# Experts' tiles of a fused attention and mixture-of-experts kernel: rows normalised one tile ahead, turned behind the second chunk, rounded in front of the activations, an expert read once on TensorE

## What is computed

```python
x = x + _L0_xattn_ref(ctx_1024, _layernorm(x), ...)
gate_scores = softmax(z @ Wg + bg)                # z = _layernorm(x)
top1 = argmax(gate_scores)                        # one expert of 8 for a token
h = silu(z @ W1[e] + b1[e])                       # 256 -> 1024
y = (h @ W2[e] + b2[e]) * gate_scores[top1]       # 1024 -> 256
x = x + y
```

## Time and profile before

| | before |
|---|---|
| runs, median (lowest to highest) | 2175.25 us (2172.24 to 2176.8) |
| profiled execution, device time | 2173.39 us |
| profiled execution, first to last instruction (span) | 2171.7 us |
| mean granted TensorE clock | 0.975 of full speed |
| busy share of the span: PE, DVE, ACT, POOL | 93%, 74%, 68%, 65% |
| first tile gathered | 1899.15 us |
| last tile's scatter begins | 2162.61 us |

### The profile page before, as it was taken

One profiled execution on the slowest core, in us unless ns is written; L12 is line 12 of the kernel. 1 busy time (PEld: TensorE's weight loads), 2 busy tenths in 40 slices (PEclk: granted clock), 3 DMA queues, 4 the chain that ended last, 5 costly groups with the idle time before them and its releaser, 6 DMA issues. The chain is left out here.

```text
span 2171.7 us, 63039 instructions
## 1 busy us (share of the span) xinstructions
PE 2010.2 (93%) x25468; PEld 1367.3 (63%) x25468; DVE 1615.2 (74%) x3115; ACT 1472.5 (68%) x1835; POOL 1421.1 (65%) x803
## 2 busy tenths in 40 slices
PE   2799999999999999999999999999999998589997
PEld 2266666667666666667666666676666665567675
DVE  7677777777778888777788887777888874745554
ACT  4277777776677777766777777767777777156664
POOL 3078888884688877865877788748878877023232
PEclk9699999999999999999999999999999999789999
DMA  5122222222222222222222222222222221271110
GB/s 167 37 53 53 53 54 63 53 55 59 68 58 54 53 53 53 59 54 70 53 58 63 54 53 53 49 71 54 62 54 54 53 62 28 94 302 37 44 44 27
DMA packets 127505, 137.92 MB, mean 64 GB/s; under 512 B 45538, under 2 KB 92310, under 8 KB 126070
## 3 DMA queue, kind: packets, MB, share of 16 engines
q1 hardware_dynamic: 123477, 124.49, 22.3%
q0 software_dynamic: 3744, 9.39, 1.4%
HBM read 53.06 MB, written 26.15 MB: 36 GB/s over the span
## 5 line engine op out<-in xcount | busy, mean ns | idle before, releaser
L708 POOL TENSOR_TENSOR probs_split<-probs,probs_split 128x1024 f16<-128x1024 f32 x576 | 1222.8, 2136 | 363.2 <-ACT probs_split L793 362.1
L786 ACT ACTIVATE probs<-score 128x1024 f32<-128x1024 f32 (+1 forms) x640 | 655.9, 1025 | 397.4 <-PE score L1076 386.8
L931 DVE TENSOR_REDUCE max_parts<-aux 128x1 f32<-128x512 f32 x1024 | 683.1, 688 | 101.7 <-PE aux L1076 93.5
L793 ACT ACTIVATE probs_split<-score 128x1024 f16<-128x1024 f32 (+1 forms) x640 | 652.0, 1019 | 0.0
L1172 PE MATMUL acc<-values,probs_split 128*128 128x65 f16 x5120 | 554.7, 193 | 8.2 <-POOL probs_split L708 8.0
L1176 PE MATMUL acc<-values,probs_split 128*128 128x64 f16 x4608 | 519.8, 194 | 0.0
L1177 PE MATMUL acc<-values,probs_split 128*128 128x65 f16 x4608 | 517.6, 192 | 0.0
L1172 PEld LDWEIGHTS acc<-values,probs_split 128*128 128x128 f16 x5120 | 464.0, 97 | 64.5 <-POOL probs_split L708 11.7
L1076 PE MATMUL score<-q_both,k_high 128*128 128x512 f16 (+1 forms) x1280 | 485.7, 379 | 10.6 <-DMA q_max<-max_row 7.8
L1076 PE MATMUL aux<-k_high,q_both 128*128 128x512 f16 (+1 forms) x1536 | 461.9, 335 | 33.0 <-DVE values L927 20.6
L1076 PE MATMUL score<-q_max,k_low 65*128 65x512 f16 (+1 forms) x1280 | 488.6, 382 | 0.0
(11 more groups left out here) (170 smaller groups left out, 2242.7 us busy)
## 6 DMA issues: line engine op xcount, KB each, us to landing
k_high<-raw SPq DMA_DIRECT2D x128, 147.2 KB, 2.5
q_both<-raw SPq DMA_DIRECT2D x128, 128.0 KB, 2.5
piece_in<-in_L_ffn_W SPq DMA_DIRECT2D x64, 256.0 KB, 3.1
halves<-piece_out SPq DMA_DIRECT2D x128, 128.0 KB, 2.4
k_low<-raw SPq DMA_DIRECT2D x64, 147.2 KB, 2.4
q_max<-raw SPq DMA_DIRECT2D x64, 128.0 KB, 2.5
w<-halves SPq DMA_DIRECT2D x16, 512.0 KB
w<-halves SPq DMA_DIRECT2D x8, 1024.0 KB
```

Source lines behind the costliest of these rows:

```text
L708: nc.gpsimd.tensor_tensor(out=low[0:r, :], in0=prob(h, j)[0:r, :], in1=high[0:r, :], op=ALU.subtract)\
L786: nc.scalar.activation(prob(h, j)[0:r, :], score[j % 2][0:r, :], ACT.Exp, scale=SCALE)\
L793: nc.scalar.activation(halves(h, j)[0][0:r, :], score[j % 2][0:r, :], ACT.Exp, scale=SCALE)\
L931: nc.vector.tensor_reduce(max_parts[g % 2][:, t, c:c + 1], bank[:, :], AX.X, ALU.max)\
```

## The change

PE turns tile `k + 2` behind chunk 1 and no longer behind chunk 4. It reads each tile's expert once, behind that `turn`, and keeps it until the tile is done: four reads to a group where five stood. ACT rounds the turned rows of `k + 2` (`z_high_half`) ahead of the first half of `hidden_layer` of `k + 1`, no longer behind it. DVE normalises tile `k + 3` and no longer `k + 2` in the step of tile `k`, and does it behind the first half of `hidden_low` of `k + 1` and right ahead of `finish` of `k`; tile 2 is normalised ahead of the loop. POOL's and SP's programs are as they were.

```diff
+    TURN_AT = 1
@@ ACT
                 hidden_layer(i, u, 1)
+                z_high_half(i, u + 2)
                 hidden_layer(i, u + 1, 0)
-                z_high_half(i, u + 2)
@@ DVE
             z_low_half(0, 1)
+            normalise_rows(0, 2)
             hidden_low(0, 0, 0)
             dve.wait_ge(b2_loaded, 16)
             def step(i, u):
                 hidden_low(i, u, 1)
-                normalise_rows(i, u + 2)
                 z_low_half(i, u + 2)
                 hidden_low(i, u + 1, 0)
+                normalise_rows(i, u + 3)
                 finish(i, u)
@@ PE
-            e = expert_of(0, 0)
+            experts_of = {0: expert_of(0, 0)}
             for c in range(KF):
-                upward(0, 0, e, c)
-            experts_of = {}
+                upward(0, 0, experts_of[0], c)
+            experts_of[1] = expert_of(0, 1)
             def step(i, u):
                 more = exists(i, u + 1)
-                if u == 0:
-                    experts_of[0], experts_of[1] = expert_of(i, 0), expert_of(i, 1)
+                k = number(i, u)
                 for c in range(KF):
                     if more:
-                        upward(i, u + 1, experts_of[u + 1], c)
-                    downward(i, u, experts_of[u], c)
-                    if c == BANK:
+                        upward(i, u + 1, experts_of[k + 1], c)
+                    downward(i, u, experts_of[k], c)
+                    if c == TURN_AT:
                         turn(i, u + 2)
-                        if u + 2 <= OWN and exists(i, u + 2):
-                            experts_of[u + 2] = expert_of(i, u + 2)
+                        if exists(i, u + 2):
+                            experts_of[k + 2] = expert_of(i, u + 2)
```

## The result

The changed kernel takes 2214.3 us (median of 4 runs, 2212.62 to 2214.76), the kernel before beside it 2174.84 us. The ratio is 1.0181, with a 95% interval from 1.0163 to 1.0198: 39 us slower. The forecast was 2221 us.

A forecast was written before the change was run, and what follows sets the result against it. PE set the pace before; a ring through DVE and the gather would now, at 7.58 us a tile. 48.2 us late at tile 35, less 2.3, gives 45.9 us on 2175.25: 2221 us, range 2205 to 2230.

The forecast's parts named there:

- The ring: DVE's finish waits behind the gather that the previous tile's outputs free; 7.58 us a tile, bounds 6.7 and 7.9.
- The sum: Ring links 0.83 + 1.32 + 3.07 + 0.95 + 1.41 = 7.58 us a tile, over PE's 6.19 us.
- The landing: Link from the gather's start on POOL to its landing: 3.07 us, the mean of 30 gathers; median 2.8.
- Normalise to finish: Link on DVE from normalise to finish's first instruction, the expert's read between: 0.95 us; other bound some 0.35 us.
- The two ends of the sum: Before the 31 links: tile 4's outputs 9.3 us late; after tile 35: some 2.3 us less than before's 16.8.
- Part one: PE, one register read fewer in four tiles: gain of 0.69 us per four tiles, some 6 us; bounds 0 to 6.
- Parts two and three: PE's turn moved behind chunk 1, and ACT's rounding ahead of the activations: each forecast to cost nothing by itself.
- Where PE would wait: PE's downward matmuls at chunk 4 stop for DVE's second half of hidden_low, about 1.4 us for each tile.
- the clock: Rival: PE's stops lower its clock, 7.8 us a tile, up to 16 us more, 2237 us; chance 0.10.
- The short ring: Rival: same ring, expert's read overlapping normalisation and fewer long landings; 6.7 to 7.3 us a tile, 2193 to 2212; chance 0.17.
- The faster and the equal case: Rivals: gather in time, 2169 us, chance 0.05; ring binds only while weights load, no difference, 2178 us, chance 0.03.

## Why the prediction came out as it did

**The cause and its sign were right.** The ring from outputs over scatter, gather, normalise and finish was forecast from the order of the code and the rows of before. DVE's order alone makes the loss, and three different ways of opening the ring (the gather first, six buffers, and finish ahead of normalising) all but end DVE's waits for the gather, to 2.1 us or less behind 1950; the last of them gives the time back only with the turn and ACT's order taken back too.

**The sum, term by term.** Outputs to scatter 0.83 forecast and 0.84 measured; scatter to gather 1.32 and 1.32; finish 1.41 and 1.40. The landing (from the gather's start to the normalisation that it releases): 7.36 less the other links of 4.32 leaves 3.04 us on average, against 3.07 forecast from the mean; the median of the changed kernel's 32 gathers from 1950 is 2.8 us, so the choice of the mean was right. Normalise to finish was the term that was mis-sized: 0.95 forecast, 0.76 measured. The row I took it from, has one more instruction between the released wait and the read, and I did not take that instruction off. The pace was 7.36 where 7.58 was forecast, and 31 x 0.22 = 6.8 us is the whole difference between 2221 and 2214.3.

The two ends of the sum held, and partly by luck. Tile 4 was done at 1959.13 - 0.83 = 1958.3 where 1958.2 was forecast, but the four landings up to it took 7.0, 6.3, 5.1 and 3.6 us, 22.0 in all, where I had 6.8, 6.8, 4.0 and 3.07, 20.7 in all; the link that was 0.19 us shorter in each of the four turns, and a tile 0 done 0.6 us earlier, made up for it. From the scatter of tile 35 to the last it took 14.4 us where 14.5 was forecast, but one reason that I gave, PE standing at chunk 4, is not what the trace shows. (4 x 6.19 in part one is 24.76 us, not 24.77, which changes nothing.)

**Part one was right:** 6 us forecast for the single reads, 7 (5 to 9) measured in a kernel where PE sets the pace, and none of it seen in the changed one.

**Parts two and three held in the sum and were incomplete as reasons.** I said that the early turn and the early rounding cost nothing by themselves. With the ring open by six buffers that holds. By POOL's order it is not shown: 0.9993 (0.9984 to 1.0002) there against 0.9968 (0.9957 to 0.9979) for the single reads alone, some 5 us less. The later tiles are 6.2 us apart in both traces; from tile 0's scatter to tile 4's it takes 34.0 us with the gather first and 31.5 with the single reads alone, and the rest of the difference stays open. But the three moves depend on each other: with DVE's finish first again, the early turn makes a ring of 7.0 us through PE, and with the turn late, the early rounding makes one of 7.05 us through ACT. The prediction named neither. The expectation of finish first named the one through PE and made it half a microsecond too short; the one through ACT was found only by its run.

**Where PE would wait was wrong.** I forecast its stop at downward's chunk 4, for hidden_low, once a tile. It stands at the turn, chunk 1: 34 times, and the wait at downward shows twice. The timeline of PE has the stop, 0.67 us and a restart, and the row that ends the tile, which is read below it:

```profile
1977.79 0.27 PE L1646 MATMUL down<-w,shared 128*128 x1
1978.73 0.44 PE L1610 MATMUL turned<-ident,shared 128*128 128x128 f32 x2 [0.67 <-DVE shared L1531]
1979.47 0.57 PE L1629 MATMUL up<-shared,w 128*128 128x128 f16 x6 [0.30 <-issue]
...
1983.54 0.27 PE L1646 MATMUL down<-w,shared 128*128 x1
```

I called tile k + 2 normalised "a step ahead". It is, in the code; in time that step ends with the very wait that the ring makes, so the rows of k + 2 are ready only 1.8 us before the outputs of k - 1 are (1985.33 + 0.41 against 1987.50). What I had said under the clock holds: PE ends a tile, six chunks behind the turn, at 1983.54 + 0.27 = 1983.81, and finish of that tile starts at 1986.09, 2.3 us later, where I had about 2. PE's busy share fell less than forecast, to 87% (190.43 us of the 220 from 1960 to 2180) and not to near 80%. The shorter tile explains part of that, and a matmul's record was longer: 0.096 us on average there, 0.091 us in the kernel before from 1960 to 2140.

**The rivals.** The short ring did not come: the read was not hidden, and moving it showed what it cost. Still, 0.76 us is a step from my 0.95 towards the 0.35 of that rival, and 2214.3 us lies only 2 us above its range. The clock did fall, but only three times behind 1960: the granted clock was 0.66 from 1965 to 1970, from 2105 to 2110 and from 2170 to 2175, each time behind a stop of PE at the turn (1.29, 2.74 and 1.19 us) for a gather that had taken 3.4, 5.0 and 3.4 us to land. Gathers as late, 3.5 us at 1996.79 and 3.4 at 2047.77, left it at 1.00. The falls cost nothing that can be seen: the turns of the ring in which PE is slow take 7.12, 7.09 and 8.14 us, which is their landings of 2.8, 2.8 and 3.8 us and the other links of 4.3. The 2.3 us between PE's end of a tile and finish are room for a slower PE. The row of PE and the window behind it, for the second fall:

```profile
2103.73 0.44 PE L1610 MATMUL turned<-ident,shared 128*128 128x128 f32 x2 [2.74 <-DVE shared L1531]
...
2105.00:2110.00 5.00, 5.00 (x42) 3.79 (x42) 2.06 (x4) 1.77 (x5) 2.00 (x2) 0.66 0.17 55
```

The faster and the equal case would have needed the gather in time for DVE, which took six buffers or the exchanged order on POOL.

## What to carry to other kernels

Before a step is moved earlier in an in-order queue, write down what it waits for and what stands behind it, and close the loop: if the step behind it releases what it waits for, the sum of the latencies over that loop is the least time of a tile, whatever the busy shares say. Such a ring is priced by adding the links from single rows, with the mean of the DMA landings and not their median; it is opened by more buffers, which spread it over more tiles, or by issuing the freed buffer's gather ahead of other DMAs. And test moves in the groups that need each other, since taking back one of three can leave a ring that was not there in either version.

## What the runs showed that I had not expected

A single instruction of sequence shows in a register read: with one more instruction between the released wait and finish the way took 0.97 us, without it 0.76 us, and 0.33 us with the read ahead of the wait. It shows only behind a wait: with six buffers, where DVE does not wait there, the same two instructions with the same read between them start 0.40 to 0.58 us apart, 0.41 in the median of 30; in the rows shown there the read begins at 1989.3, half a microsecond ahead of the normalisation.

Issued first behind its wait, the gather takes longer on POOL: median 1378 ns (1177 to 1386) over 30 gathers, where it takes 975 to 979 ns behind a scatter in the kernels before and changed; the scatter behind it is unchanged at 1018 ns. No run tells why.

```profile
L1394 POOL DMA_INDIRECT shared<-x,read_i x30: 1177/1378/1386, 1958.2 to 2137.5; - x30
```
